# The first round of q and k projections of a fused attention and expert block, re-staged on five engines

## The chip, the cores and the metric

The kernel runs on one core of one Trainium2 chip, as a single launch. The metric is device time in microseconds from start to end of one execution; the figure of a version is the median of its runs.

## What is computed

The reference is a transformer block on 16 batches of 1024 tokens with 256 features, cut here to what matters:

```python
qkv = x @ Wqkv                                   # q, k, v: 16 heads of 16
for i in range(H):
    cos, sin = tables(i)                         # each head has its own frequencies
    q_rot, k_rot = rotary(q[:, i], cos, sin), rotary(k[:, i], cos, sin)
    att = einsum('btd,bsd->bts', q_rot, k_rot) * scale
    if i: att = att + cascade_w[i - 1] * cascade_bias
    att = softmax(where(causal, -inf, att))
    head_outputs.append(einsum('bts,bsd->btd', att, v[:, i]))
    cascade_bias = mean(att, axis=1, keepdims=True)
x = layernorm(x + concatenate(head_outputs) @ Wproj)
x = layernorm(x + mixture_of_8_experts(x))       # top 1, sigmoid weight, silu gate
```

## The kernel before

**The units.** The 256 pairs of batch and head are units. They run head after head in groups of four batches (four slots). A unit is eight steps; step by step TensorE fills scores twice (`fill_a`, `fill_b`), VectorE takes row maxima (`row_max`, L942), ScalarE takes exponentials (`exp_a`, `exp_b`), TensorE multiplies with v (`att_v`) and GpSimd works on short columns.

**The projections.** Scores come from bfloat16 stacks: q and k are each split into three bfloat16 parts, whose six products are laid one under the other in `q_stack` and `k_stack`. Eight heads of four batches make one round of projections: 16 chunks of 128 features by 512 tokens (four a batch: two of q, two of k) and eight value jobs. One chunk n goes through these stages, each named in `chunk_job`:

- `qk_a`, `qk_b` (L706, TensorE): the two halves of the product over 256 features, into a PSUM bank.
- `qk_turn` (L978 and L979, VectorE): times the cosine table into `by_cos`, and neighbouring rows exchanged into `swapped`. It frees the bank.
- `qk_sin` (L1292 and L1296, GpSimd): `swapped` times the sine table, plus `by_cos`, into one of two halves of `rotated`.
- `qk_first` (L839 on ScalarE in the first round): the first bfloat16 part.
- `qk_less` (L985, VectorE): the remainder, into one of two halves of `resid`.
- `qk_second` (L991, VectorE): the second part, a cast.
- `qk_third` (L1305, GpSimd): the third part.
- `qk_send` (L1438, queue of SP): the three parts to `qk_parts` in DRAM, from one of three buffers of `parts`.

**What sets the order.** The function `timetable` lays the stages of all jobs out in steps before a kernel instruction is made. A stage comes `gap` steps after the one before it in its job, not before those named in `after`, and, if it holds a bank, not before one is free. Each engine then issues its share of the steps in order, so a wait holds up whatever stands behind it on that engine. The first round is laid out before the units, in the steps up to `PROLOGUE`, with no unit beside it; the later rounds go between the units' steps, a chunk at a time. In the first round `by_cos` and `swapped` are single, and `qk_turn` of a chunk waits for `qk_sin` of the chunk before.

**The first stacks.** At step `PROLOGUE` SP waits until all 16 sends have landed and issues 12 loads of 16 by 4096 elements for head 0 (`load_stack`, L1375), and four short loads of zeros behind them (L1379). The first `fill_a` (L623) waits for all of these.

**The loads at the start.** SP issues 14 constants, `w_qkv` second among them (L1346), then x of batches 1 and 0 (L1431) and the cosine and sine tables. All constants count on one semaphore, which the first projection waits for. Two rooms hold x: batches 2 and 3 wait for the projections of batches 0 and 1.

## Time and profile before

| | us |
|---|---|
| median of three runs | 4006.76 |
| lowest and highest run | 4002.16, 4019.21 |
| profiled execution, its own time | 4015.91 |
| its span in the trace | 4014.0 |
| TensorE busy | 3248.6 (81%) |
| ScalarE busy | 3127.4 (78%) |
| VectorE busy | 2632.2 (66%) |
| GpSimd busy | 2175.5 (54%) |
| mean granted TensorE clock | 0.942 of full speed |

The profile cuts the span into 40 slices and gives the busy share of each engine in tenths: PE (TensorE) and ACT (ScalarE) show 5388888 and 1399999 in the first seven, so the first two slices, some 200 us, differ from what follows. The trace gives times from the start of the span. A row of its timeline has start, duration, engine, line, operation, and in brackets the idle time before and what ended it; DVE is VectorE, POOL GpSimd, and SPq an issue on SP's queue.

### The profile page before, as it was taken

What the parts mean: (1) busy time and instruction counts of PE and PEld (TensorE: products, weight loads), DVE (VectorE), ACT (ScalarE), POOL (GpSimd) and SP (SyncE); (2) the same over time, 40 slices, a digit from 0 to 9 for tenths busy, and PEclk for the clock granted to TensorE, in tenths of its full rate; (3) what the DMA queues carried; (4) which work ended last, traced back from release to release, by engine and by line L of the source; (5) the groups of instructions that cost most, each with busy time, mean ns of one, the idle gap of its engine ahead of it and who ended that gap; (6) DMA issues with size and microseconds to landing.
All of it is one profiled execution on the core that took longest, in us unless ns stands there. A gap on an engine that the chain in (4) does not pass through costs nothing. (4 is left out here: it accounts for less than half of the span.)

```text
span 4014.0 us, 86383 instructions
## 1 busy us (share of the span) xinstructions
PE 3248.6 (81%) x26666; PEld 1728.4 (43%) x26666; DVE 2632.2 (66%) x7958; ACT 3127.4 (78%) x8883; POOL 2175.5 (54%) x6232
## 2 busy tenths in 40 slices
PE   5388888888888788888888878888888888888756
PEld 2144434444444444444444434444444444444444
DVE  3466665666777667666767666667676766776546
ACT  1399999998788877778877877778887888888534
POOL 4555555555555466664554456665654534654227
PEclk8699999999999999999999999999998999999977
DMA  3333223333333433433442333443433423444245
GB/s 103 88 75 69 69 65 69 76 76 72 96 85 101 95 100 94 105 97 90 103 101 78 101 78 90 105 115 100 95 92 75 110 59 72 105 106 93 84 151 164
DMA packets 217693, 371.30 MB, mean 93 GB/s; under 512 B 45077, under 2 KB 160541, under 8 KB 204944
## 3 DMA queue, kind: packets, MB, share of 16 engines
q1 hardware_dynamic: 201872, 327.91, 32.8%
q0 software_dynamic: 15360, 37.87, 3.6%
q8 instruction: 213, 3.49, 0.4%
q14 instruction: 248, 2.03, 0.2%
HBM read 261.86 MB, written 104.92 MB: 91 GB/s over the span
## 5 line engine op out<-in xcount | busy, mean ns | idle before, releaser
L942 DVE CUSTOM_DVE_ANT_0 att_a<-scores,window 128x128 f32<-128x128 f32 (+7 forms) x2048 | 1495.1, 755 | 977.2 <-PE scores L623 700.8
L808 ACT ACTIVATE att_a<-att_a,neg_max 128x128 f32<-128x128 f32 (+7 forms) x2048 | 1576.8, 770 | 390.8 <-DVE neg_max L942 382.6
L818 ACT ACTIVATE att_t<-scores 128x1024 f32<-128x1024 f32 (+7 forms) x2048 | 1306.5, 638 | 175.8 <-PE scores L642 164.5
L640 PE MATMUL scores<-q_stack,k_stack 102*128 102x512 bf16 (+3 forms) x3072 | 833.4, 340 | 441.5 <-DVE neg_max L942 261.4
L666 PE MATMUL pv<-att_t,v_sb 128*32 128x128 f32 (+1 forms) x13312 | 893.3, 328 | 31.8 <-DVE o_sb L957 21.2
L623 PE MATMUL scores<-k_stack,q_stack 99*128 99x512 bf16 (+3 forms) x3072 | 697.7, 337 | 95.1 <-DMA k_stack<-in_zeros 59.8
L666 PEld LDWEIGHTS pv<-att_t,v_sb 128*32 128x32 f32 x13312 | 473.3, 111 | 463.0 <-issue 230.4
L640 PEld LDWEIGHTS scores<-q_stack,k_stack 102*128 102x128 bf16 x3072 | 243.6, 99 | 916.0 <-DVE neg_max L942 619.3
L642 PE MATMUL scores<-identb,mask 128*128 128x128 bf16 x2048 | 461.0, 225 | 0.0
L818 ACT ACTIVATION_READ_ACCUMULATOR att_t<-scores 128x1 f32 x2048 | 402.0, 196 | 0.1
L623 PEld LDWEIGHTS scores<-k_stack,q_stack 99*128 99x128 bf16 x3072 | 252.2, 100 | 336.0 <-issue 182.3
L808 ACT ACTIVATION_READ_ACCUMULATOR att_a<-att_a,neg_max 128x1 f32 x2048 | 390.3, 191 | 0.0
L1250 POOL TENSOR_SCALAR guess<-row_sum 128x8 f32<-128x8 int32 x256 | 51.4, 201 | 623.0 <-ACT att_a L808 612.8
L1292 POOL TENSOR_TENSOR swapped<-swapped,sine 128x512 f32<-128x512 f32 x128 | 162.9, 1273 | 293.4 <-DVE swapped L979 293.4
L706 PE MATMUL side<-xT,w_qkv 128*128 128x512 f32 x460 | 257.8, 643 | 19.2 <-DMA xT<-in_xt 15.3
L642 PEld LDWEIGHTS scores<-identb,mask 128*128 128x128 bf16 x2048 | 204.8, 100 | 100.0 <-issue 48.0
L1336 POOL DMA_INDIRECT out<-runner_r,out_id x140 | 145.5, 1039 | 101.9 <-DVE runner_r L1218 52.8
L1305 POOL TENSOR_TENSOR parts<-resid,parts 128x512 bf16<-128x512 f32 x128 | 153.3, 1199 | 73.0 <-DVE parts L991 72.7
L1329 POOL DMA_INDIRECT runner_r<-x_rows,in_id x140 | 142.4, 1017 | 77.9 <-DVE out_id L1175 36.7
L1296 POOL TENSOR_TENSOR rotated<-swapped,by_cos 128x512 f32<-128x512 f32 x128 | 163.1, 1274 | 33.1 <-DVE resid L985 14.8
L1300 POOL TENSOR_SCALAR parts<-rotated 128x512 bf16<-128x512 f32 x112 | 168.6, 1506 | 9.1
L792 PE MATMUL side<-runner_r 128*128 128x128 f32 x1040 | 154.2, 294 | 17.7 <-DVE runner_r L1200 6.2
(339 smaller groups left out, 4304.6 us busy)
## 6 DMA issues: line engine op xcount, KB each, us to landing
runner_r<-in_experts SPq DMA_DIRECT2D x140, 384.0 KB, 4.0
qk_parts<-parts SPq DMA_DIRECT2D x128, 384.0 KB, 3.1
q_stack<-qk_parts SPq DMA_DIRECT2D x384, 128.0 KB
k_stack<-qk_parts SPq DMA_DIRECT2D x384, 128.0 KB
xT<-in_xt SPq DMA_DIRECT2D x30, 1024.0 KB
head_out<-o_sb SPq DMA_DIRECT2D x252, 64.0 KB, 2.1
x_rows<-finisher_f SPq DMA_DIRECT2D x28, 514.0 KB, 4.0
finisher_f<-head_out SPq DMA_DIRECT2D x56, 256.0 KB, 4.7
```

What stands on the lines that cost most here:

```text
L623: made = engine.matmul(scores[:, c0:c1], qs[0:ROWS_A, i * P:(i + 1) * P], ks[0:ROWS_A, c0 - base:c1 - base], start=True, stop=True)
L640: engine.matmul(scores[:, c0:c1], ks[0:ROWS_B, j * P:(j + 1) * P], qs[0:ROWS_B, j * P + c0 - base:j * P + c1 - base], start=True, stop=True)
L642: engine.matmul(scores[:, base:base + P], mask[:, :], identb[:, :], start=False, stop=True, skip_group_check=True).then_inc(s_b_filled, 1)
L666: made = engine.matmul(dst, lhsT, src, start=(j == 0), stop=(p == TB - 1), skip_group_check=True)
L706: made = engine.matmul(room, w_qkv[:, k, col:col + P], xT[x_room(m)[0]][:, k, c % 2 * WB:(c % 2 + 1) * WB], start=(k == 0), stop=(k == KT ...
L792: made = engine.matmul(room[:, two * P:(two + 1) * P], r.w_gu[:, k, two, :], r.xwT[:, k * P:(k + 1) * P], start=(k == 0), stop=(k == KT - 1))
L808: engine.activation(taken, taken, EXP, scale=-1.0, bias=neg_max[:, n, i:i + 1], accum_out=row_sum[:, n, i:i + 1]).then_inc(s_exp_a, 1)
L818: engine.activation(att_t[:, ring:ring + end - base], scores[:, base:end], EXP, accum_out=col_sum[:, n, j:j + 1]).then_inc(s_exp_b, 1)
L942: engine.tensor_tensor_reduce(out=att_a[:, ring:ring + end - base], in0=scores[:, base:end], in1=window[:, T - (end - base):T], op0=ALU.ad ...
L1292: ev = small(engine.tensor_tensor(swapped[:, :], swapped[:, :], sine[:, cols], ALU.mult))
L1296: engine.tensor_tensor(rotated[:, b, :], swapped[:, :], by_cos[:, :], ALU.add).then_inc(s["qk_sin"], 1)
L1300: engine.tensor_scalar(parts[:, n % NPARTS, 0, :], rotated[:, n % 2, :], SCALE if n // 2 % 2 == 0 else 1.0, None, ALU.mult).then_inc(s["qk ...
```

## The change

It touches the first round alone and what stands around it. `first_chunk_job` replaces `chunk_job` for the first 16 chunks: gaps of one and no phases, and `qk_turn` of chunk n waits for `qk_sin` of n-2. A second pair of buffers for `by_cos` and `swapped` lies in `att_t`, which the first `exp_b` would otherwise write. The third part moves from GpSimd to VectorE, the second from VectorE to ScalarE. The loads of x move to ScalarE's queue. On SP, `w_qkv` comes first with a semaphore of its own and the other constants follow the tables; the zeros are loaded early; head 0's stacks are loaded batch by batch, each set as 12 loads of 16 by 1024 elements. Ones in the stacks are written as float32 pairs, and the scaling of `w_cas` moves to the end of the prologue.

```diff
+    def first_chunk_job(n):
+        return [Stage("qk_a", n, 0, hold=3, after=(("x_load", n // 4), ("tables", 0), ("qk_b", n - 1))),
+                Stage("qk_b", n, 1),
+                Stage("qk_turn", n, 1, frees=True, after=(("qk_sin", n - 2),)),
+                Stage("qk_sin", n, 0, after=(("qk_less", n - 2),)),
+                Stage("qk_first", n, 1, after=(("qk_send", n - NPARTS),)),
+                Stage("qk_less", n, 1), Stage("qk_second", n, 1), Stage("qk_third", n, 1), Stage("qk_send", n, 0)]
...
+        turn_bufs = [(by_cos[:, :], swapped[:, :]), (att_t[:, 0:WB], att_t[:, WB:2 * WB])]
+        def turn_buf(n):
+            return turn_bufs[n % 2 if n < 4 * SLOTS else 0]
...
-                    pe.wait_ge(s_stack[h % 2], 192 * (hh // 2 + 1))
+                    if hh == 0:
+                        pe.wait_ge(s_first[slot], 192)
+                    else:
+                        pe.wait_ge(s_stack[h % 2], 192 * (hh // 2 + h % 2))
...
-                            pe.wait_ge(s_loaded, ALL_LOADED)
+                            pe.wait_ge(s_w_qkv, 16)
...
+                    elif kind == "qk_second" and t < PROLOGUE:
+                        act.wait_ge(s["qk_less"], nth["qk_less", n])
+                        engine.copy(parts[:, n % NPARTS, 1, :], resid[:, n % 2, :]).then_inc(s["qk_second"], 1)
+                    elif kind == "x_load" and t < PROLOGUE:
+                        load_x(act, engine, n)
...
-            dve.wait_ge(s_loaded, ALL_LOADED)
-            engine.tensor_scalar(w_cas[:, :], w_cas[:, :], 1.0 / T, None, ALU.mult).then_inc(s_set_up, 1)
...
+                if t == PROLOGUE:
+                    dve.wait_ge(s_loaded, ALL_LOADED)
+                    engine.tensor_scalar(w_cas[:, :], w_cas[:, :], 1.0 / T, None, ALU.mult).then_inc(s_set_up, 1)
...
-                        if n:
-                            dve.wait_ge(s["qk_sin"], nth["qk_sin", n - 1])
+                        was = n - 2 if n < 4 * SLOTS else n - 1
+                        if was >= 0:
+                            dve.wait_ge(s["qk_sin"], nth["qk_sin", was])
...
-                    elif kind == "qk_second":
+                    elif kind == "qk_third" and t < PROLOGUE:
+                        dve.wait_ge(s["qk_second"], nth["qk_second", n])
+                        engine.tensor_tensor(parts[:, n % NPARTS, 2, :], resid[:, n % 2, :], parts[:, n % NPARTS, 1, :],
+                                             ALU.subtract).then_inc(s["qk_third"], 1)
+                    elif kind == "qk_second" and t >= PROLOGUE:
...
+            def load_first_stack(slot):
+
+                for b in range(NPARTS):
+                    sp.wait_ge(s_parts[b], 16 * len(range(b, 4 * (slot + 1), NPARTS)))
+                for n in range(2 * PRODUCTS):
+                    qk, k = divmod(n, PRODUCTS)
+                    stack, part = ((q_stack, Q_PARTS[k]), (k_stack, K_PARTS[k]))[qk]
+                    engine.dma_start(stack[k * HD:(k + 1) * HD, 0, slot, :],
+                                     qk_parts[qk, part, 0:HD, slot, :]).then_inc(s_first[slot], 16)
...
-                if t == PROLOGUE:
-                    for n in range(2 * PRODUCTS + SLOTS):
-                        load_stack(0, n)
+                if t == 1:
+                    load_constants()
+                    sp.wait_ge(s_set_up, READY)
+                    for slot in range(SLOTS):
+                        load_zeros(0, slot)
...
+                        if m < SLOTS and slot and c == 1:
+                            load_first_stack(slot - 1)
+                        if n == 4 * SLOTS - 1:
+                            load_first_stack(slot)
```

On VectorE in the steady part of the first round a chunk stands as these rows before (the turn of chunk 4, the cast of chunk 1, the remainder of chunk 2, and so on):

```order
L978 TENSOR_TENSOR by_cos<-scores,cosine 128x512 [waits s_qk_sin,s_qk_b]
L979 STREAM_SHUFFLE swapped<-scores 128x512
L991 CAST parts<-resid 128x512 [waits s_qk_less]
L985 SCALAR_TENSOR_TENSOR resid<-rotated,parts 128x512 [waits s_qk_third,s_qk_first]
L978 TENSOR_TENSOR by_cos<-scores,cosine 128x512 [waits s_qk_sin,s_qk_b]
L979 STREAM_SHUFFLE swapped<-scores 128x512
L991 CAST parts<-resid 128x512 [waits s_qk_less]
L985 SCALAR_TENSOR_TENSOR resid<-rotated,parts 128x512 [waits s_qk_third,s_qk_first]
```

and as these now (the turn of chunk 4, the third part of chunk 1, the remainder of chunk 3), with two pairs of buffers:

```order
L1018 TENSOR_TENSOR by_cos<-scores,cosine 128x512 [waits s_qk_sin,s_qk_b]
L1019 STREAM_SHUFFLE swapped<-scores 128x512
L1030 TENSOR_TENSOR parts<-resid,parts 128x512 [waits s_qk_second]
L1025 SCALAR_TENSOR_TENSOR resid<-rotated,parts 128x512 [waits s_qk_third,s_qk_first]
L1018 TENSOR_TENSOR att_t<-scores,cosine 128x512 [waits s_qk_sin,s_qk_b]
L1019 STREAM_SHUFFLE att_t<-scores 128x512
L1030 TENSOR_TENSOR parts<-resid,parts 128x512 [waits s_qk_second]
L1025 SCALAR_TENSOR_TENSOR resid<-rotated,parts 128x512 [waits s_qk_third,s_qk_first]
```

The remainder now stands one chunk nearer to the turn behind it, the third part is in the place of the cast, and the turn's wait is for a sum on GpSimd that lies one chunk further back.

On GpSimd the same stretch reads before:

```order
L1305 TENSOR_TENSOR parts<-resid,parts 128x512 [waits s_qk_second]
L1292 TENSOR_TENSOR swapped<-swapped,sine 128x512 [waits s_qk_turn]
L1296 TENSOR_TENSOR rotated<-swapped,by_cos 128x512 [waits s_small,s_qk_less]
L1305 TENSOR_TENSOR parts<-resid,parts 128x512 [waits s_qk_second]
L1292 TENSOR_TENSOR swapped<-swapped,sine 128x512 [waits s_qk_turn]
L1296 TENSOR_TENSOR rotated<-swapped,by_cos 128x512 [waits s_small,s_qk_less]
```

and now:

```order
L1337 TENSOR_TENSOR swapped<-swapped,sine 128x512 [waits s_qk_turn]
L1341 TENSOR_TENSOR rotated<-swapped,by_cos 128x512 [waits s_small,s_qk_less]
L1337 TENSOR_TENSOR att_t<-att_t,sine 128x512 [waits s_qk_turn]
L1341 TENSOR_TENSOR rotated<-att_t 128x512 [waits s_small,s_qk_less]
L1337 TENSOR_TENSOR swapped<-swapped,sine 128x512 [waits s_qk_turn]
L1341 TENSOR_TENSOR rotated<-swapped,by_cos 128x512 [waits s_small,s_qk_less]
```

The subtraction that stood ahead of each product is gone from this engine.

On SP the end of the first round, from the last sends to the next round's x and tables, reads before:

```order
L1438 DMA qk_parts<-parts 128x3x512 [waits s_qk_third] x16
L1375 DMA q_stack<-qk_parts 16x4096 [waits s_parts1,s_parts2,s_parts0,s_set_up]
L1375 DMA q_stack<-qk_parts 16x4096 x5
L1375 DMA k_stack<-qk_parts 16x4096 x6
L1379 DMA k_stack<-in_zeros 3x1024 x4
L1431 DMA xT<-in_xt 128x2x1024 [waits s_qk_b,s_v_b]
L1422 DMA cosine<-in_cos 128x1024 [waits s_qk_sin]
L1423 DMA sine<-in_sin 128x1024
```

and now, from the four sends ahead of the third batch's stack on:

```order
L1494 DMA qk_parts<-parts 128x3x512 [waits s_qk_third] x4
L1438 DMA q_stack<-qk_parts 16x1024 [waits s_parts2,s_parts1,s_parts0]
L1438 DMA q_stack<-qk_parts 16x1024 x5
L1438 DMA k_stack<-qk_parts 16x1024 x6
L1494 DMA qk_parts<-parts 128x3x512 [waits s_qk_third] x2
L1438 DMA q_stack<-qk_parts 16x1024 [waits s_parts2,s_parts1,s_parts0]
L1438 DMA q_stack<-qk_parts 16x1024 x5
L1438 DMA k_stack<-qk_parts 16x1024 x6
L829 DMA xT<-in_xt 128x2x1024 [waits s_qk_b,s_v_b]
L1484 DMA cosine<-in_cos 128x1024 [waits s_qk_sin]
L1485 DMA sine<-in_sin 128x1024
```

The loads of batches 0 to 2 stand between sends, and those of batch 3 are left between the last send and the next x.

## Rows read from the trace of the kernel before

**Rows 1.** the page: the span

```profile
span 4014.0 us, 86383 instructions
```

**Rows 2.** busy by stretch: PE, PEld, DVE, ACT, POOL; clock, DMA share

```profile
57.00:131.00 74.00, 17.63 (x37) 6.90 (x36) 31.64 (x61) 8.90 (x15) 49.39 (x37) 0.58 0.21 69
...
200.00:600.00 400.00, 344.02 (x2957) 161.45 (x2956) 242.54 (x663) 375.97 (x1079) 227.30 (x751) 1.00 0.30 70
```

**Rows 3.** timeline, one chunk of the steady stretch: start us, us, what

```profile
65.49 0.69 DVE L978 TENSOR_TENSOR by_cos<-side,cosine 128x512 f32<-128x512 f32 x1 [3.74 <-POOL rotated L1296]
...
66.10 0.72 DVE L979 STREAM_SHUFFLE swapped<-side 128x512 f32<-128x512 f32 x1
...
67.04 0.69 DVE L985 SCALAR_TENSOR_TENSOR resid<-rotated,parts 128x512 f32<-128x512 f32 x1
67.21 1.53 POOL L1305 TENSOR_TENSOR parts<-resid,parts 128x512 bf16<-128x512 f32 x1 [1.82 <-DVE parts L991]
...
68.71 1.26 POOL L1292 TENSOR_TENSOR swapped<-swapped,sine 128x512 f32<-128x512 f32 x1
...
70.11 1.26 POOL L1296 TENSOR_TENSOR rotated<-swapped,by_cos 128x512 f32<-128x512 f32 x1
71.40 0.63 ACT L839 ACTIVATE parts<-rotated 128x512 bf16<-128x512 f32 x1 [5.35 <-POOL rotated L1296]
71.47 0.69 DVE L978 TENSOR_TENSOR by_cos<-scores,cosine 128x512 f32<-128x512 f32 x1 [3.74 <-POOL rotated L1296]
```

**Rows 4.** timeline, SP's issues and the first scores

```profile
132.87 2.65 SPq L1375 DMA_DIRECT2D q_stack<-qk_parts  x6
...
139.70 0.40 SPq L1431 DMA_DIRECT2D xT<-in_xt  x1
...
147.30 1.33 PE L623 MATMUL scores<-k_stack,q_stack 99*128 99x128 bf16 x4 [59.82 <-DMA k_stack<-in_zeros]
147.60 0.29 DVE L942 CUSTOM_DVE_ANT_0 att_a<-scores,window 128x128 f32<-128x128 f32 x1 [18.55 <-PE scores L623]
```

**Rows 5.** timeline, the first x load, projection and turn

```profile
7.94 0.47 SPq L1431 DMA_DIRECT2D xT<-in_xt  x1
...
15.35 2.07 PE L706 MATMUL side<-xT,w_qkv 128*128 128x512 f32 x2 [15.35 <-DMA xT<-in_xt]
...
20.88 0.69 DVE L978 TENSOR_TENSOR by_cos<-side,cosine 128x512 f32<-128x512 f32 x1 [2.46 <-PE side L706]
```

**Rows 6.** timeline, TensorE in batch 0 and the load of batch 3

```profile
28.81 1.05 PE L720 MATMUL scores<-w_qkv,att_a 128*128 128x128 f32 x8
...
30.60 1.02 PE L706 MATMUL side<-xT,w_qkv 128*128 128x512 f32 x2
...
44.73 0.38 SPq L1431 DMA_DIRECT2D att_a<-in_xt  x1
...
50.73 1.16 PE L720 MATMUL scores<-w_qkv,att_a 128*128 128x128 f32 x8 [3.50 <-DMA att_a<-in_xt]
```

**Rows 7.** timeline, VectorE behind GpSimd, and GpSimd alone

```profile
122.53 1.44 POOL L1292 TENSOR_TENSOR swapped<-swapped,sine 128x512 f32<-128x512 f32 x1
...
122.77 1.75 DVE L985 SCALAR_TENSOR_TENSOR resid<-rotated,parts 128x512 f32<-128x512 f32 x1
...
129.13 1.15 POOL L1305 TENSOR_TENSOR parts<-resid,parts 128x512 bf16<-128x512 f32 x1 [1.09 <-DVE parts L991]
```

**Rows 8.** one line of the kernel: ns least, median, most

```profile
L978 DVE TENSOR_TENSOR by_cos<-side,cosine x117: 672/685/692, 20.9 to 3213.4; 128x512 f32<-128x512 f32 x117
```

**Rows 9.** DMA issues up to 180 us: KB, median us from issue to landing

```profile
qk_parts<-parts SPq DMA_DIRECT2D x16, 384.0 KB, 2.5
...
cosine<-in_cos SPq DMA_DIRECT2D x2, 512.0 KB, 9.7
```

**Rows 10.** timeline, the first projection of the second round

```profile
158.48 3.24 PE L706 MATMUL side<-xT,w_qkv 128*128 128x512 f32 x4
...
163.28 0.69 DVE L978 TENSOR_TENSOR by_cos<-side,cosine 128x512 f32<-128x512 f32 x1
```

More of the change, by code:

```diff
@@ L87, in block_kernel @@
     NEG = 4
+    TWO_ONES = float(np.array([0x3f803f80], np.uint32).view(np.float32)[0])
     SWAP = [i ^ 1 for i in range(32)]
@@ L287, in timetable @@
             for c in range(4):
-                begin(chunk_job(4 * slot + c))
+                begin(first_chunk_job(4 * slot + c))
             for c in range(2):
@@ L548, in block_kernel @@
         s_stack = [signal(f"s_stack{i}") for i in range(2)]
+        s_first = [signal(f"s_first{i}") for i in range(SLOTS)]
         s_shift = [signal(f"s_shift{i}") for i in range(SLOTS)]
@@ L1291, in pool_program @@
                         pool.wait_ge(s_tables, 32 * (n // 16 + 1))
-                        ev = small(engine.tensor_tensor(swapped[:, :], swapped[:, :], sine[:, cols], ALU.mult))
+                        straight, crossed = turn_buf(n)
+                        ev = small(engine.tensor_tensor(crossed, crossed, sine[:, cols], ALU.mult))
                         if n >= 2:
@@ L1295, in pool_program @@
                         pool.wait_ge(s_small, ev)
-                        engine.tensor_tensor(rotated[:, b, :], swapped[:, :], by_cos[:, :], ALU.add).then_inc(s["qk_sin"], 1)
+                        engine.tensor_tensor(rotated[:, b, :], crossed, straight, ALU.add).then_inc(s["qk_sin"], 1)
                     elif kind == "qk_first" and t >= PROLOGUE:
```

70 lines of the change are left out of this document (38 added, 32 removed).

## The prediction

> **What bounds the kernel now.** The span is 4014.0 us [rows 1]. I read the table by stretch first, because the change touches only the start: between 200 and 600 us ScalarE is busy for 376 of 400 us [rows 2], so the units pace themselves, and what they gain or lose at their start moves their end by as much. Between 57 and 131 us no engine is full: VectorE is busy for 31.6 of 74 us, GpSimd for 49.4 [rows 2]. A stretch like that is a chain of waits, so I then read the timeline of one chunk.
>
> The chain repeats every 5.98 us, from the product with cosine at 65.49 to the next at 71.47 [rows 3]. By the starts: product with cosine 0.61, exchange and cast until GpSimd's subtraction begins 1.11, subtraction 1.50, product with sine 1.40, sum 1.36 until VectorE may write `by_cos` again. The sum is 5.98, and everything in it stands in a row because there is one `by_cos`. VectorE's idle time of 3.74 us ahead of each product with cosine is that wait.
>
> At the end of the round SP issues the stacks from 132.87, the first scores start at 147.30, held by the last landing, and the first row maximum at 147.60 [rows 4]. The number to predict is this last one, called R. It is 147.6 now.
>
> **Start.** x of batch 0 is issued at 7.94 behind 14 constants; the first product starts with its landing at 15.35 and the first turn at 20.88 [rows 5]. Now `w_qkv` and x head two queues. The wait can shrink by no more than the 7.2 us by which the issue comes sooner, (7.94 to about 0.7), and could grow by 0.8 if bytes in flight set it: by the shapes 3.7 MB land up to 15.35 now, and 3.9 with the tables ahead and the other constants behind. The queue's 14 short issues are gone either way; I take 2.35 us, a third of the upper end. Ones as float32 pairs and `w_cas` at the end cost nothing: VectorE waits for TensorE there, 2.46 us before the first turn [rows 5]. If that cover went, it would still have the 5 us of the first projection.
>
> **TensorE's lead, chunks 0 to 3.** Two halves of value jobs lie between 28.81 and 30.60 [rows 6], 0.9 us each, which is 1.05 less the overlap with the next; half a projection is 1.02 less the same, 0.86, so four chunks with two value jobs are 8 x 0.86 + 4 x 0.9 = 10.5 us, or 2.6 a chunk. Projection 3 ends at 31.62 [rows 6], now at 29.3. Its turn takes 1.35 us (0.61 and 0.72 [rows 3]) and its sum is ready 2.7 us after that: 33.4. Up to there TensorE sets the pace. x of batch 2 is asked for at 29.4, and its first use comes behind turns that aren't due before 37.
>
> **Chunks 4 to 15.** With two pairs of buffers the turn of n+2 runs beside the sum of n+1. What remains is a ring of three engines, and its pace has these bounds:
> - GpSimd alone: 1.40 + 1.26 us and the start of the next, some 2.7; TensorE's 2.6 is just under it. So 2.75 a chunk is the lower bound.
> - The two engines hinder each other. VectorE's remainder takes 0.69 us [rows 3] and 1.75 when it starts 0.24 us into a GpSimd product [rows 7]; GpSimd's subtraction takes 1.15 us alone [rows 7] and 1.53 when it starts inside the remainder [rows 3]. Either waits for most of what the other has left. The product with cosine, which reads PSUM, shows 692 ns at most over 117 [rows 8], so I let it and the exchange run free. No row shows the third part on VectorE; its nearest is the remainder, the same size with one more operation, 0.69. Two such operations a chunk, with 0.1 to 0.2 us saved at each hand-over, put 1.0 us on 2.7: **3.7 us**.
> - `parts` has three buffers. From the remainder of n+1 to that of n+3 there are turn 1.35, remainder and third part 0.69 each, a send of 2.6 (2.5 from issue to landing [rows 9]), and the first part 0.63 with 0.1 of signals: 6.1 us for two chunks, 3.05 each, and up to 4.1 if both VectorE operations wait 1.06 us.
>
> I take 3.7, which both of the last two allow. Moving the cast to ScalarE removes nothing further: its copy is the size of the first part, 0.63, and ScalarE has two such a chunk. Twelve chunks give 33.4 + 12 x 3.7 = 77.8.
>
> x of batch 3 took 6.0 us from issue to first use [rows 6]. Now it is asked for after projection 7, near 42.5, which waits for a turn; it lands at 48.5 and projection 9 is done at 50.4. Its sum would begin at 51.9 by the pace. The load is hidden by 1.5 us, and not if the pace is quicker.
>
> SP issues 12 stack loads in some 5.3 us (six in 2.65 [rows 4]). Three times this stands between sends: each time the next send comes 5.8 - 3.7 = 2.1 us late, of which 0.7 to 1.1 are slack. I take 1 us each, 3 in all, between 0 and 6. So the sum of chunk 15 is ready at 80.8.
>
> Behind it come first part 0.63, remainder 0.69, second 0.6, third 0.69 and four signals: 3.1. R is **83.9**, 63.7 us sooner. The 14.4 us of stack loads that stood ahead of R are now behind it for batch 3 alone and beside other work for the rest.
>
> **What comes late next.** SP is left with the last stack's 12 issues and the landing ahead of it, so x and tables of the next round are issued 8.0 us after R; they were issued at 139.70, 7.9 us ahead of it. TensorE first wants that x at 158.48 and VectorE the table at 163.28 [rows 10], 10.9 and 15.7 us after R. With a landing of 5.5 and, for the tables, 9.7 us [rows 9], they come 2.6 and about 2.3 late. Behind TensorE's wait stand the scores of unit 1, behind VectorE's its row maxima; the two waits overlap. I charge 3 us, between 0 and 10. The fourth stack lands some 13 us after R, and unit 3 starts later than 20. TensorE's clock is 0.58 in the stretch to 131 [rows 2] and the four halves at 158.48 take 3.24 us; it might be up sooner after a shorter idle time, worth 0 to 3 us. I count none.
>
> **Sum.** 63.7 - 3.0 = 60.7 us. On the profiled execution that is 4015.9 - 60.7 = 3955.2; that one lay 9.2 us above the median of 4006.8, and by the median the forecast is **3946**. The difference is 1.5%, three times the half per cent (20 us) that a measurement of this kernel can tell.
>
> A rule speaks against two engines so closely paired. The Trainium skill (SBUF — State Buffer, "Who interferes with whom") says that a VectorE operation with two inputs in SBUF and a GpSimd operation that reads SBUF exclude each other for the whole instruction. The 1.75 us agree with it; by the letter of it a chunk would cost 1.26 + 1.26 + 0.69 + 0.69 = 3.9 us. The loads of x gain little by another rule of the Trainium skill (DMA: Bandwidth & Descriptors, "Issuing engines are not separate DMA queues"): a second queue saves issue time only. By it the start gains what the constants free, as charged.
>
> **The rivals.**
> - *Nothing overlaps at a hand-over.* The pace is 3.9, the four durations one behind the other. For it: 1.75 is a whole remainder plus 1.06 of waiting. Against: the product it waited for had 1.20 us left [rows 7], so 0.14 were saved. 12 x 0.2 = 2.4 later: 3949. Chance 0.15. The Trainium skill's page on SBUF says the same.
> - *The engines hardly meet.* The remainder falls into GpSimd's gap and the pace is 2.8. Then x of batch 3 is no longer hidden: sum 9 at 54.4, sum 15 at 71.2, R at 74.3, and 3937. Against: GpSimd would have no gap left. Chance 0.15.
> - *The ring of `parts` sets the pace.* Both VectorE waits and sends slowed behind stack loads give 4.6: 33.4 + 55.2 + 3.1 = 91.7, a gain of 55.9 - 3, so 3954; with next-round loads later by 7 us more, 3961. For it: twelve loads issued from 132.87 on had landed only by 147.30 [rows 4]. Chance 0.13.
> - *One chunk in flight, slower than before.* If the sends' landing closed the ring so that a chunk's whole chain of turn 1.35, product and sum 2.7, first 0.7, remainder 1.75, second 0.65, third 1.75, send 2.6, some 11.5 us, ran alone, R would be 18.5 + 16 x 11.5 = 202 and the kernel 4061. It decides from a pace of 8.5 us on. Against it stand two turn pairs, two halves of `rotated`, three of `parts`. Chance 0.02.
> - *The change doesn't carry through.* R comes early, but the units wait for something tied to the start of the span, and the time stays near 4000. No row shows such a thing. Chance 0.05.
>
> **How the numbers follow.** The forecast has 0.50, with 3938 to 3955 as its own range. The range of 3928 to 3964 takes in the quick pace less a clock gain, the ring with late loads, and 3 us of scatter; left out are the last two rivals and the far ends. Faster by over 0.5% is every case down to 3986.7: 0.50 + 0.15 + 0.15 + 0.13 = 0.93, and 0.01 of the last: 0.94. Same 0.04, slower 0.02.
>
> **What would show it.** First turn at 18.5; products with cosine 3.7 us apart from chunk 4 on; VectorE's remainders and third parts well over 0.69 us; the first row maximum at 84; the first projection of the second round waiting for x some 11 us behind it; the stretch beyond 200 us unchanged, only earlier. The forecast is wrong if the spacing is under 3.0 or over 4.5, or if units 1 to 4 lose over 10 us.

## The result, and the profile after it

| | before | changed |
|---|---|---|
| median, us | 4012.99 (4 runs) | 3959.61 (4 runs) |
| lowest and highest | 4002.16, 4022.01 | 3958.26, 3960.26 |
| profiled execution, its span | 4015.91, 4014.0 | 3960.26, 3958.5 |
| first row maximum, R | 147.60 | 84.45 |
| from R to the end of the span | 3866.4 | 3874.1 |

The ratio is 0.9868, with a 95% interval of 0.9839 to 0.9897: 1.3% faster, and the interval does not reach 1. One run more of the kernel before moved its median from 4006.76 to 4012.99, so the medians are 53.4 us apart and the two profiled spans 55.5. Of those spans the prologue gave 147.60 - 84.45 = 63.15 us, and what follows R took 7.65 back.

The busy times of the changed kernel, from the page:

```profile
PE 3240.7 (82%) x26666; PEld 1725.4 (44%) x26666; DVE 2638.1 (67%) x7958; ACT 3135.6 (79%) x8899; POOL 2159.7 (55%) x6216
```

They hardly differ from before: the work is the same. The difference lies in when it runs. Three stretches of the changed kernel follow, the first the pipeline, the second what stands right behind R, the third the one that [rows 2] shows for the kernel before. The columns are the stretch, its length, the busy time of each engine, the granted clock, the DMA share and GB/s.

```profile
20.00:76.90 56.90, 42.11 (x180) 24.96 (x179) 43.74 (x71) 19.96 (x36) 45.70 (x30) 0.89 0.42 134
84.45:110.00 25.55, 11.05 (x24) 3.06 (x24) 11.54 (x34) 11.65 (x29) 3.19 (x17) 0.50 0.46 143
200.00:600.00 400.00, 342.50 (x2929) 160.18 (x2928) 241.81 (x661) 373.05 (x1071) 224.41 (x744) 0.99 0.30 68
```

In the pipeline VectorE and GpSimd are now busy for 77% and 80% of the time, where they were at 43% and 67%. Behind R, TensorE works for 11 of 25.6 us. Beyond 200 us ScalarE again has 373 of 400 us: that stretch is unchanged, only earlier.

**The start.** These are rows of the timeline of the changed kernel: start, duration, engine, line, operation, and the idle time before with what ended it. They answer to [rows 5].

```profile
0.73 0.48 ACTq L829 DMA_DIRECT2D att_a<-in_xt  x1
1.25 0.52 ACTq L829 DMA_DIRECT2D xT<-in_xt  x1
14.48 2.08 PE L727 MATMUL side<-xT,w_qkv 128*128 128x512 f32 x2 [14.48 <-DMA xT<-in_xt]
20.00 0.69 DVE L1018 TENSOR_TENSOR by_cos<-side,cosine 128x512 f32<-128x512 f32 x1 [10.26 <-PE side L727]
```

The load of x that goes out first is that of batch 1, into `att_a`; batch 0, which TensorE waits for, stands behind it. The first product is 0.87 us sooner than before, though its x is asked for 6.7 us sooner. Nine kernels of this document have this start; their first products lie between 13.81 and 14.48 and their first turns between 18.48 and 20.00, so the trace shown is at the late end of both.

**One chunk.** The same view of VectorE and GpSimd in the steady part. It answers to [rows 3].

```profile
68.40 0.68 DVE L1018 TENSOR_TENSOR att_t<-side,cosine 128x512 f32<-128x512 f32 x1
...
69.01 0.72 DVE L1019 STREAM_SHUFFLE att_t<-side 128x512 f32<-128x512 f32 x1
...
69.63 0.67 DVE L1030 TENSOR_TENSOR parts<-resid,parts 128x512 bf16<-128x512 f32 x1
69.81 1.61 POOL L1337 TENSOR_TENSOR att_t<-att_t,sine 128x512 f32<-128x512 f32 x1 [0.21 <-DVE att_t L1019]
...
70.40 1.57 DVE L1025 SCALAR_TENSOR_TENSOR resid<-rotated,parts 128x512 f32<-128x512 f32 x1
71.57 1.53 POOL L1341 TENSOR_TENSOR rotated<-att_t 128x512 f32<-128x512 f32 x1
71.90 0.68 DVE L1018 TENSOR_TENSOR by_cos<-scores,cosine 128x512 f32<-128x512 f32 x1
```

The next turn comes 3.50 us after this one, and VectorE's rows carry no idle time. The remainder (L1025) takes 1.57 us where it took 0.69; it starts 0.59 into GpSimd's product with sine (L1337) and ends 0.55 after it. The product itself takes 1.61; with the third part (L1030) it shares 0.5 us. By the starts the chain is: turn 0.61, exchange and its signal 0.80, product 1.61, what the remainder has left after it 0.48. The sum is 3.50. The product for one chunk and the remainder of the chunk before stand in one row, though neither needs the other's result. This holds from the turn of chunk 4 on. The turns of chunks 1 to 3 are 3.5 us apart too, but for another reason. There VectorE is idle and waits for TensorE, for 2.17, 1.58 and 0.26 us:

```profile
23.52 0.69 DVE L1018 TENSOR_TENSOR att_t<-scores,cosine 128x512 f32<-128x512 f32 x1 [2.17 <-PE scores L727]
...
27.02 0.69 DVE L1018 TENSOR_TENSOR by_cos<-scores,cosine 128x512 f32<-128x512 f32 x1 [1.58 <-PE scores L727]
```

TensorE is busy without a gap from 20.0 to 30.5 us, with two halves of a projection (0.86 each) and two halves of value jobs (0.89 each) for every chunk, which makes 3.5 us.

**Behind the last send.** The issues on SP's queue in the changed kernel, and what waits for them. They answer to [rows 4] and [rows 10].

```profile
82.74 2.95 SPq L1438 DMA_DIRECT2D q_stack<-qk_parts  x6
85.74 2.73 SPq L1438 DMA_DIRECT2D k_stack<-qk_parts  x6
88.51 0.95 SPq L1494 DMA_DIRECT2D qk_parts<-parts  x2
92.51 2.63 SPq L1438 DMA_DIRECT2D q_stack<-qk_parts  x6
95.18 2.73 SPq L1438 DMA_DIRECT2D k_stack<-qk_parts  x6
98.02 0.39 SPq L829 DMA_DIRECT2D xT<-in_xt  x1
```

```profile
84.45 0.28 DVE L977 CUSTOM_DVE_ANT_0 att_a<-scores,window 128x128 f32<-128x128 f32 x1
...
102.90 3.78 PE L727 MATMUL side<-xT,w_qkv 128*128 128x512 f32 x4 [8.01 <-DMA xT<-in_xt]
```

The last two sends have their data by 84.5, yet they go out at 88.51, behind the 12 issues of batch 2's stack. Only when they have landed, at 92.5, do the last 12 go out, and x of the next round behind those, at 98.02, 13.6 us after R. The sends are 4.1 us late by that, and their own issue and landing take 4.0. TensorE waits 8.01 us for x, and the first projection of the second round starts 18.45 us after R instead of 10.9.

### The profile page after: what moved, and what is told of

Its sections match the earlier page's. It is cut to its first block and busy times, and to the rows that moved or that the text cites. A ratio compares the mean times of both kernels' runs of the same rounds, so it can differ in the third digit from the quotient of the medians.

```text
span 3958.5 us, 86418 instructions
## 1 busy us (share of the span) xinstructions
PE 3240.7 (82%) x26666; PEld 1725.4 (44%) x26666; DVE 2638.1 (67%) x7958; ACT 3135.6 (79%) x8899; POOL 2159.7 (55%) x6216
## 3 DMA queue, kind: packets, MB, share of 16 engines
q8 instruction: 213, 3.49, 0.4%
## 5 line engine op out<-in xcount | busy, mean ns | idle before, releaser
L1337 POOL TENSOR_TENSOR swapped<-swapped,sine 128x512 f32<-128x512 f32 x120 | 154.8, 1290 | 302.6 <-DVE swapped L1019 302.6
L977 DVE DVE_READ_ACCUMULATOR2_ANT neg_max<- 128x1 f32 x2048 | 168.2, 82 | 0.0
L1341 POOL TENSOR_TENSOR rotated<-swapped,by_cos 128x512 f32<-128x512 f32 x120 | 154.2, 1285 | 17.2
```

The costliest lines, as they stand in the source:

```text
L977: engine.tensor_tensor_reduce(out=att_a[:, ring:ring + end - base], in0=scores[:, base:end], in1=window[:, T - (end - base):T], op0=ALU.ad ...
L1337: ev = small(engine.tensor_tensor(crossed, crossed, sine[:, cols], ALU.mult))
```

## The experiments

Two theories stood against each other. **Theory A** was that of the forecast: VectorE and GpSimd hold each other up and so set the pace, and the late x is what the kernel gives back. **Theory B** had two parts: the pace is that of the sends' ring of `parts` or of the stack loads between the sends, and the time lost after R comes from the batch-wise stacks themselves.

Kernels 1 to 4 ran on one chip, where the kernel before took 4013.52 us; 5 to 8 on a second, where its one run took 4086.15; 9 to 11 on a third, where it took 4062.71. The pace repeats on all three, to some 0.02 us. R scatters more: the unchanged change has 84.45 and 83.61, and kernel 1, whose issues are the same up to its last send, has 81.79. So the pace is compared across all, a difference in R of less than 3 us between two kernels shows nothing, and whole times are compared only with the kernel before on the same chip. Kernels 2 to 8 have one time each.

### 1. x of the next round ahead of the last stack

```diff
                         if n == 4 * SLOTS - 1:
+                            load_x(sp, engine, SLOTS)
+                            load_tables(1)
                             load_first_stack(slot)
```

> The x and the two tables of the second round are issued on SP between the last send and the last stack, instead of behind it. Theory (the units lose 7.6 us after the first row maximum, because TensorE waits 8.0 us for this x with the scores of unit 1 queued behind it): the first row maximum stays at 84.5, the second round's first projection starts 10 to 12 us behind it instead of 18.4, and the span falls by 6 to 8 us against the changed kernel, to about 3951. Rival (the units would have lost the time anyway, to a low TensorE clock or to the late fourth stack): the projection starts sooner, but the span falls by less than 2 us.

R was 81.79 and not 84.5: its first turn came at 18.48, and the rest lies within the scatter. The issue of x and the projection in this kernel's timeline:

```profile
87.26 0.38 SPq L829 DMA_DIRECT2D xT<-in_xt  x1
...
93.24 2.08 PE L727 MATMUL side<-xT,w_qkv 128*128 128x512 f32 x2 [1.03 <-DMA xT<-in_xt]
```

TensorE's wait falls from 8.01 to 1.03 us, and the projection starts 11.45 us after R. To see what that is worth I took the GpSimd operation that ends each unit's row sums (`guess`), here of unit 8, in the kernel before, the changed one and this one:

```profile
263.81 0.20 POOL L1250 TENSOR_SCALAR guess<-row_sum 128x8 f32<-128x8 int32 x1
```

```profile
210.31 0.20 POOL L1294 TENSOR_SCALAR guess<-row_sum 128x8 f32<-128x8 int32 x1
```

```profile
200.93 0.20 POOL L1294 TENSOR_SCALAR guess<-row_sum 128x8 f32<-128x8 int32 x1
```

Counted from R these are 116.2, 125.9 and 119.1 us. The change lost 9.7 us there, and the order of two loads and a stack gives back 6.8 of them. The median was 3954.59 us (3943.21 to 3964.20), a ratio to before of 0.9841 [0.9816, 0.9867], whose interval overlaps that of the change. So the mechanism is shown at unit 8, and the gain in whole time by this edit alone is not. Its profiled execution was the slowest of the four. By unit 96 the 6.8 us, counted from R, have shrunk to 0.9, while two executions of the unchanged change (the second is kernel 11) differ by 3.6 there. TensorE's granted clock falls in some stretches among the units, as to 0.83 between 320 and 340 us here, 0.85 there in the changed kernel and 0.91 between 480 and 500 in the kernel before. I put the loss of the lead down to such stretches, which is argued and not tested.

### 2. Stacks loaded whole, behind all sends

```diff
+                if t == PROLOGUE:
+                    for n in range(2 * PRODUCTS):
+                        load_stack(0, n)
...
-                        if m < SLOTS and slot and c == 1:
-                            load_first_stack(slot - 1)
-                        if n == 4 * SLOTS - 1:
-                            load_first_stack(slot)
```

> Head 0's stacks are again loaded whole, 12 loads of 16 by 4096, behind all 16 sends; everything else as changed. Theory (the pace of 3.5 us is set by VectorE and GpSimd, and the stack loads between sends cost about 1 us each and 4 to 5 in all): turns stay 3.5 us apart from chunk 4 to 15, the last third part is ready about 4 us sooner, near 80, and the first row maximum comes 17 us behind it, near 97, 13 us later than now. Rival (the ring of three send buffers sets the pace of itself): turns are 3.9 apart even without stack loads, and the first row maximum is near 101.

```profile
84.60 2.63 SPq L1420 DMA_DIRECT2D q_stack<-qk_parts  x6
...
99.30 0.29 DVE L974 CUSTOM_DVE_ANT_0 att_a<-scores,window 128x128 f32<-128x128 f32 x1 [17.57 <-PE scores L641]
```

R is 99.30, 14.9 us later than with the batch-wise loads. The pace stays at 3.50, and the last turn comes at 74.19 instead of 77.00. From first turn to last it is 54.36 us, against 57.00, 56.40 and 55.86 in the three executions with batch-wise stacks (the changed kernel, kernels 11 and 1): the 36 issues between the sends cost 1.5 to 2.6 us. Without them the turns of chunks 9 and 10 still come 1.6 us late in all, behind a TensorE that waits 3.47 us for x of batch 3. Unit 8 ends its row sums 117.4 us after R. But x of the next round is issued ahead of R here, as in the kernel before, so this kernel alone can't tell the stacks from the late x. Kernel 9 can: it has batch-wise stacks, four loads at a time, and x in time, and nothing is lost after R. The one time was 3973.35 us.

### 3. The third part almost left out

The third part is computed for 8 of its 512 columns and is zero in the others, so its time on VectorE goes and everything else stays.

```diff
-                        engine.tensor_tensor(parts[:, n % NPARTS, 2, :], resid[:, n % 2, :], parts[:, n % NPARTS, 1, :],
+                        engine.tensor_tensor(parts[:, n % NPARTS, 2, 0:8], resid[:, n % 2, 0:8], parts[:, n % NPARTS, 1, 0:8],
```

> In the first round the third part is taken of 8 of 512 columns only, the others are left zero, so VectorE has one two-input operation a chunk instead of two. Theory (in the steady part VectorE and GpSimd take the SBUF port in turn, and VectorE is never free: products 0.61, exchange 0.62, third part 0.78, remainder 1.50 with its wait, 3.5 in all): the product with sine starts 0.35 sooner and takes 1.26 instead of 1.61, and the pace falls to 2.8 to 2.9 us, where TensorE sees to it that it falls no further. Rival (send ring or signals): the pace stays over 3.3.

```profile
66.51 0.68 DVE L1019 TENSOR_TENSOR att_t<-side,cosine 128x512 f32<-128x512 f32 x1
...
67.75 0.14 DVE L1031 TENSOR_TENSOR parts<-resid,parts 128x8 bf16<-128x8 f32 x1
67.92 1.26 POOL L1338 TENSOR_TENSOR att_t<-att_t,sine 128x512 f32<-128x512 f32 x1 [0.21 <-DVE att_t L1020]
...
68.41 1.32 DVE L1026 SCALAR_TENSOR_TENSOR resid<-rotated,parts 128x512 f32<-128x512 f32 x1 [0.52 <-ACT parts L871]
...
69.66 0.68 DVE L1019 TENSOR_TENSOR by_cos<-scores,cosine 128x512 f32<-128x512 f32 x1
```

The pace is 3.15, between what the two theories gave. VectorE lost 0.53 us of work and now idles for 0.52, so its own load no longer sets the pace. The product fell from 1.61 to 1.26, and the pace by the same 0.35: turn 0.61, exchange and signal 0.80, product 1.26, rest of the remainder 0.48. The third part thus costs the pipeline 0.35 us a chunk, and only through GpSimd's product. R was 81.47, only 3 us sooner and hardly outside the scatter: some chunks took 4.56, and the first three gaps stayed at 3.5 to 3.9, as they would where TensorE sets them. The one time was 3953.41 us.

### 4. One pair of turn buffers

```diff
         def turn_buf(n):
-            return turn_bufs[n % 2 if n < 4 * SLOTS else 0]
+            return turn_bufs[0]
```

with `qk_turn` waiting for `qk_sin` of n-1 again, in the stage list and in VectorE's wait.

> One pair of turn buffers instead of two, with the wait for the sum of the chunk before, and all else as changed. Theory (the second pair is the main part of the gain in pace): the ring is product 0.61, exchange and third part 1.3, sine and sum 2.7 with a port wait of 0.35, and 0.1 of signals, 5.0 us a chunk, so the first row maximum comes 12 x 1.4 = 17 us later, near 101. Rival (moving the subtraction off GpSimd was the main part): the pace is under 4.3 us and the first row maximum before 95.

```profile
60.68 0.69 DVE L1018 TENSOR_TENSOR by_cos<-side,cosine 128x512 f32<-128x512 f32 x1 [1.23 <-POOL rotated L1341]
...
62.10 1.61 POOL L1337 TENSOR_TENSOR swapped<-swapped,sine 128x512 f32<-128x512 f32 x1 [1.52 <-DVE swapped L1019]
...
63.85 1.53 POOL L1341 TENSOR_TENSOR rotated<-swapped,by_cos 128x512 f32<-128x512 f32 x1
...
65.49 0.69 DVE L1018 TENSOR_TENSOR by_cos<-scores,cosine 128x512 f32<-128x512 f32 x1 [1.23 <-POOL rotated L1341]
```

The chain is that of [rows 3] without GpSimd's third part: 1.42 + 1.75 + 1.64 = 4.81 a chunk. R was 96.96, 12.5 later than with two pairs; the one time was 3970.86 us. The expectation had 5.0 and an R of 101. In this order the parts that the change moves to other engines take 1.17 us off the chunk of before (5.98 to 4.81), and the second pair takes off 1.31 more (to 3.50).

### 5. The third part back on GpSimd

```diff
-                    elif kind == "qk_third" and t >= PROLOGUE:
+                    elif kind == "qk_third":
```

on GpSimd, and VectorE's branch for it taken out.

> The third part of the first round goes back to GpSimd; two turn pairs and all else as changed. Theory (engines take the port in turn): GpSimd has 1.15 + 1.26 + 1.36 of its own and waits for most of a remainder of 0.69, so the pace is 4.2 to 4.5 us instead of 3.5, and the first row maximum comes 9 to 12 us later, near 95. Rival (no port, only GpSimd's own work): 3.8 us, near 88.

```profile
70.79 0.69 DVE L1025 SCALAR_TENSOR_TENSOR resid<-rotated,parts 128x512 f32<-128x512 f32 x1 [3.97 <-POOL parts L1346]
...
71.40 0.68 DVE L1018 TENSOR_TENSOR by_cos<-scores,cosine 128x512 f32<-128x512 f32 x1
...
72.81 1.26 POOL L1333 TENSOR_TENSOR swapped<-swapped,sine 128x512 f32<-128x512 f32 x1 [2.12 <-DVE swapped L1019]
74.22 1.27 POOL L1337 TENSOR_TENSOR rotated<-swapped,by_cos 128x512 f32<-128x512 f32 x1
...
75.44 1.16 POOL L1346 TENSOR_TENSOR parts<-resid,parts 128x512 bf16<-128x512 f32 x1
...
76.70 0.69 DVE L1025 SCALAR_TENSOR_TENSOR resid<-rotated,parts 128x512 f32<-128x512 f32 x1 [3.97 <-POOL parts L1346]
```

The pace is 5.91 and R 111.45: nearly that of before, with two turn pairs. What I expected added durations and overlooked an order. The remainder of chunk n overwrites `resid`, so it waits for the third part of n-2. On GpSimd that stands behind the sum, the turn stands behind the remainder on VectorE, and the product needs the turn. One file: remainder 0.61, turn and exchange with the signal 1.41, product 1.41, sum 1.22, third part 1.26. That is 5.91, and no operation is slowed by another here. The one time was 4050.67 us, 35.5 under the one run of the kernel before on this chip. So the second pair of buffers gives next to nothing to the pace without the move of the third part.

Yet R is 36.2 us sooner than before. Only 1.4 of them come at the first turn and 0.7 in the ten chunks after the sixth turn. 17.7 us lie behind the last turn, where the whole stacks stood, and 16.3 between the first and the sixth turn. These last come from a stop in the kernel before, whose turns of chunks 4 and 5 are 16.8 us apart:

```profile
56.22 0.58 ACT L848 COPY v_sb<-scores 128x512 f32<-128x512 f32 x1 [11.81 <-PE scores L720]
...
57.37 0.69 DVE L985 SCALAR_TENSOR_TENSOR resid<-rotated,parts 128x512 f32<-128x512 f32 x1 [13.03 <-ACT parts L839]
```

ScalarE waits for values of batch 3, whose x TensorE has only at 50.73 ([rows 6]), and the first parts and all behind them wait with it. In the new layout of the first round this stop is gone, here as in the changed kernel. Which edit of the layout ended it was not tested.

### 6. The cast back on VectorE

```diff
-                    elif kind == "qk_second" and t < PROLOGUE:
-                        act.wait_ge(s["qk_less"], nth["qk_less", n])
-                        engine.copy(parts[:, n % NPARTS, 1, :], resid[:, n % 2, :]).then_inc(s["qk_second"], 1)
...
-                    elif kind == "qk_second" and t >= PROLOGUE:
+                    elif kind == "qk_second":
```

> The second part of the first round goes back to VectorE as a cast, the third part stays there. In the changed kernel VectorE is without a gap in the steady part, so the cast adds its 0.33 to 0.41 us and, where it meets a GpSimd operation, up to 1 us of waiting: a pace of 3.9 to 4.5 and a first row maximum 5 to 12 us later. The prediction held that moving it removes nothing; by that the pace stays 3.5.

```profile
70.91 1.61 POOL L1334 TENSOR_TENSOR att_t<-att_t,sine 128x512 f32<-128x512 f32 x1 [1.88 <-DVE att_t L1016]
71.32 1.48 DVE L1032 CAST parts<-resid 128x512 bf16<-128x512 f32 x1
...
72.66 1.26 POOL L1338 TENSOR_TENSOR rotated<-att_t 128x512 f32<-128x512 f32 x1
72.72 1.75 DVE L1022 SCALAR_TENSOR_TENSOR resid<-rotated,parts 128x512 f32<-128x512 f32 x1
```

The cast takes 1.48 us inside GpSimd's product; in the chunk of [rows 3] it starts at 66.72 and takes 0.41. Behind it the remainder meets the sum and takes 1.75. VectorE now waits out both of GpSimd's operations, and the pace is 4.90, over the 3.9 to 4.5 that I had expected. R was 97.23, the one time 4030.56 us (55.6 under before). Moving the cast to ScalarE is worth 12.8 us of R, as much as the second pair of buffers.

### 7. x of batch 0 first

```diff
-                        load_x(act, engine, n)
+                        load_x(act, engine, 1 - n if n < 2 else n)
```

> Of the first two loads of x, that of batch 0 is issued first, and that of batch 1 behind it. Theory (bytes in flight set the landing, 1 MB takes 2.5 to 3 us at 360 to 400 GB/s): the first product starts near 11.8 instead of 14.5, the first turn near 17.5, and the first row maximum 2 to 2.7 us sooner. Rival (w_qkv is what the first product waits for, or a fixed delay): within 1 us of 14.5.

```profile
8.68 2.07 PE L727 MATMUL side<-xT,w_qkv 128*128 128x512 f32 x2 [8.68 <-DMA xT<-in_xt]
```

The first product starts at 8.68 instead of 14.48, the first turn at 14.00 instead of 20.00, more than I had expected (11.8 and 17.5). R is 78.31, 5.3 and 6.1 us under the two of the unchanged change, so what the start gains reaches R. The one time was 4020.24 us, 65.9 under before.

### 8. Stack loads four at a time

```diff
-                        if m < SLOTS and slot and c == 1:
-                            load_first_stack(slot - 1)
+                        if m < SLOTS and slot and c:
+                            load_first_stack(slot - 1, 4 * (c - 1), 4 * c)
```

> The 12 loads of each of the first three stacks are issued four at a time behind three sends instead of all at once. Theory (SP's 5.6 us of issues hold the next send back, and with three buffers the first part of a chunk then waits): turns 9 to 15 stay 3.5 to 3.6 us apart, and the first row maximum comes 3 to 4 us sooner, near 81. Rival (the loads slow the sends in the DMA engines, whoever issues them when): the same stretches, less than 1.5 us sooner.

The last turn comes at 73.44 and R at 80.89, 3.6 us sooner than in the change. From first turn to last it is 54.00 us, 1.9 to 3.0 less than with the loads all at once; the rest of the 3.6 is scatter of the start. x of the next round is issued at 92.50, still behind the last stack, and TensorE waits 6.14 us. The one time was 4020.00 us, 66.2 under before.

### 9 to 11. All three together, and the change again

Kernel 9 has the edits of 1, 7 and 8. Kernel 10 has them too, with x of the next round already behind send 13:

```diff
+                        if n == 13:
+                            load_x(sp, engine, SLOTS)
```

Kernel 11 is the changed kernel again, without an edit.

> Three edits on the changed kernel together: x of batch 0 ahead of batch 1, stack loads four at a time behind three sends, and x and tables of the second round ahead of the last stack. If the terms add, as the engines' order lets them (5.5 us at the start, 3.5 of the held sends, 7 to 9 of the late x): first row maximum near 75.5, unit 8 another 7 us or more sooner against it, and a span 15 to 18 us under the changed kernel's on the same chip. Rival (clock dips of TensorE in the units take back what the start gives): the first row maximum and unit 8 come sooner as said, but the medians differ by less than 8 us.

> As the one before, with the second round's x issued after send 13 instead of 15. Theory (in that one x comes just in time or 1 us late): the second round's first projection doesn't wait for x any more, and the tables are then what is late, so unit 8 gains 0 to 2 us more. Rival (1 MB in the DMA engines between the sends holds sends 14 and 15 back): the first row maximum comes 2 to 3 us later, and no gain is left.

> The changed kernel as it is, on the same chip as the two before, so that the medians can be compared. By both theories the first row maximum is at 84 to 85 and the ratio to the kernel before is 0.985 to 0.989.

| | R | projection after R | TensorE's wait | unit 8 | median, us | ratio to before [95%] |
|---|---|---|---|---|---|---|
| 9, all three | 76.22 | 10.7 | 0.28 | 192.4 | 3995.14 | 0.9830 [0.9812, 0.9848] |
| 10, x earlier | 75.49 | 10.2 | none | 194.0 | 3994.04 | 0.9828 [0.9812, 0.9844] |
| 11, the change | 83.61 | 18.5 | 8.06 | 208.4 | 4015.74 | 0.9878 [0.9857, 0.9898] |

The projection of the second round in the timeline of kernel 9, whose x is issued at 82.03:

```profile
86.94 2.93 PE L727 MATMUL side<-xT,w_qkv 128*128 128x512 f32 x3 [0.28 <-DMA xT<-in_xt]
```

Kernels 9 and 10 are 20.6 and 21.7 us under the change on the same chip, and their intervals against the kernel before do not meet that of the change. In kernel 9 unit 8 stands at R + 116.2, where the kernel before had it too: 7.4 us of R and 8.6 after it make 16.0. The other 5 are within the scatter. With the still earlier x of kernel 10 R is 0.7 us sooner, which is within its scatter, and unit 8 is at R + 118.5; the two can't be told apart by their times. In both the first turn now waits for the table of sines, which lands after x.

## Why the prediction came out as it did

**Right: what bounded the kernel, and what the change takes away.** R was forecast for 83.9 and came at 84.45; the gain of the prologue was put at 63.7 and is 63.15. ScalarE's share beyond 200 us did not move, as the argument from [rows 2] had it. Of the 63.15 us, 0.9 come at the first turn, 20.8 between the first and the sixth turn (where the kernel before has the stop shown under 5), 20.6 in the ten chunks after it and 20.8 behind the last turn.

That R was met within 0.55 us is in part luck, since misses cancel. The sum of chunk 3 was forecast for 33.4 and is ready at 35.25, 1.85 late. The twelve chunks behind it take 46.4 us instead of 47.4: the pace gives 2.4 and the stops take 1.4. The end from the last sum to R is 2.76 instead of 3.1.

**Start: the term was rather large.** It was put at 2.35 us. In the trace shown it is 0.87 to the first product and 0.88 to the first turn; over the nine kernels with this start it is 0.9 to 1.5 and 0.9 to 2.4 (the kernel before has one trace). The forecast took a third of the upper end by choice. Neither bound saw the cause: I read the change as x at the head of a queue, and it is x of batch 1 that is at the head. Kernel 7 shows that 5.1 to 5.8 us more were there for a swap.

A rule of the Trainium skill (DMA: Bandwidth & Descriptors, "Issuing engines are not separate DMA queues") says that a second issuing engine saves only the time of issuing. By it the start could gain at most the 6.7 us by which x is issued sooner. The trace agrees, with 0.87. The swap within one queue is worth several times as much.

**Pace: right in size, and the sum behind it wrong in one term.** It was put at 3.7 from the fourth chunk on and is 3.50. The forecast built it on GpSimd's two operations plus 1.0 for the two VectorE operations that meet them. The rows show a ring: turn, exchange, product, rest of the remainder. The third part acts in it only by the 0.35 us that it puts on the product, as kernel 3 shows. TensorE sets the pace up to chunk 3, as the forecast had it, but at 3.5 us a chunk and not at 2.6: the sum counted four halves of value jobs for four chunks, and the trace has eight. R did not feel this, because the forecast took the end of projection 3 from its row in [rows 6]. Over all 16 chunks and eight value jobs 2.6 is the mean.

**The cast: wrong.** "Moving the cast to ScalarE removes nothing further" priced the copy on ScalarE and not what the cast would cost on VectorE. Kernel 6 gives the price of leaving it: 1.40 us a chunk. It had been cheap in the kernel before, where nothing ran on GpSimd beside it (GpSimd's idle time of 1.82 us in [rows 3]).

**Left out: the move of the third part.** I counted it as a cost, one more VectorE operation that meets GpSimd. Kernel 5 shows that without it the second pair of buffers gains 0.07 us a chunk. The forecast came out because the change does both, and that is luck as far as this term goes.

**Rivals of the pace.** *Nothing overlaps*, 3.9: near in kind. VectorE's two and GpSimd's two operations do alternate without a gap, and three times a chunk one starts inside the other. The remainder meets 1.02 us of the product and takes 1.57 where 0.69 + 1.02 would be 1.71; the product meets 0.49 of the third part and loses 0.35; the sum meets 0.40 of the remainder and loses 0.27. That saves 0.14, 0.14 and 0.13, and 3.90 - 0.41 is 3.49. *The engines hardly meet*, 2.8: never, the closest is 3.15 with the third part out. *The ring of `parts`*, 4.6: it shows at single places, as in the row below, but does not set the steady pace.

```profile
59.08 0.63 ACT L871 ACTIVATE parts<-rotated 128x512 bf16<-128x512 f32 x1 [3.26 <-DMA qk_parts<-parts]
```

*One chunk in flight*: the turns are 3.5 us apart, so two or more were in flight throughout.

The Trainium skill (SBUF — State Buffer, "Who interferes with whom") says that a VectorE operation with two inputs in SBUF and a GpSimd operation that reads SBUF contend for a port that one of them holds alone, and counts a cast among those that may contend. The cast's 1.48 and the remainder's 1.57 us agree in kind. In size the waits of [rows 7] and of the chunk shown are some 0.14 us shorter than a full wait.

**Loads.** The stack issues between sends were put at 3 us, between 0 and 6: kernel 2 gives 1.5 to 2.6. x of batch 3 was forecast for issue at 42.5 and first use without a wait as long as the pace was 3.7. It was issued at 43.67, and TensorE waited for it:

```profile
49.23 1.16 PE L741 MATMUL side<-w_qkv,att_a 128*128 128x128 f32 x8 [3.02 <-DMA att_a<-in_xt]
```

The turns of chunks 10 and 11 come 4.66 and 4.93 us after those before them. The first of these waited for TensorE and so for x; the second comes with the row of the ring above, whose send stood behind the stack issues of 50.73:

```profile
56.48 0.69 DVE L1018 TENSOR_TENSOR by_cos<-scores,cosine 128x512 f32<-128x512 f32 x1 [1.06 <-PE scores L727]
```

The turn of chunk 15 comes 5.10 after the one before. Together that is 4.2 us over the pace, of which kernel 2 keeps 1.6 for x of batch 3. The prediction had said that the load is no longer hidden if the pace is quicker.

**The term that was mis-sized: "What comes late next".** I charged 3 us, between 0 and 10, and 7.65 were lost over the whole span, 9.7 by unit 8. The mechanism was the one named: x of the next round stands behind the last stack on SP. Its size was off, since the forecast had x issued 8.0 us after R and it was issued 13.6 after. I had counted the last stack's issues and a landing, and not the stack before, whose 12 issues start at 82.74, in front of sends 14 and 15. They hold the sends until 88.51, where their data is there by 84.5, and everything behind them is late by as much: 4.1 of the 5.6 us. Most of the rest is the landing of those sends, 4.0 from issue where I had some 2.7. I had priced those issues only where they hold the chunks up, not where they hold up the end of the queue. Kernel 1 shows that this was the cause: with x issued 5.5 us after R instead of 13.6, TensorE's wait is 1.03 us.

The other kernels bear it out, 3 to 6 among them, which are not in the table. Counted from R, what unit 8 loses follows how late the projection is, and some 0 to 3 us are left over:

| kernel | projection later than before, us | unit 8 later than before, us |
|---|---|---|
| changed | 7.6 | 9.7 |
| 11, the change again | 7.6 | 8.6 |
| 7 | 8.4 | 9.5 |
| 8 | 5.7 | 6.6 |
| 1 | 0.6 | 2.9 |
| 2 | 0.0 | 1.2 |
| 9 | -0.2 | 0.0 |
| 10 | -0.7 | 2.2 |

**The clock.** I counted nothing for it, between 0 and 3 gained. In the 25.55 us behind R the changed kernel shows a granted clock of 0.50, that is the lower level of 1.2 GHz, where the kernel before has 0.67, and the four halves of the first projection take 3.78 us where [rows 10] has 3.24. So it was a small loss. The idle time of 8 us is not needed for it: kernel 1 waits only 1.03 us and has 0.52 and 3.78 as well. From R to unit 8 TensorE is busy for 94.2 us in the changed kernel and 94.6 in kernel 1, against 91.8 before and 91.6 in kernel 9. That is as much as most of what is left over in the table, but kernel 11 has 92.0 there beside a rest of 1.0, so this cause is likely and not shown.

**The time.** In spans the gain was forecast at 60.7 us and is 55.5: 0.55 missed at R, and 4.65 behind it. On the profiled execution that is 3955.2 against 3960.26. By the median it was 3946 against 3959.61, 13.6 us late. The other 8.5 have no mechanism: the profiled execution of before lay 9.2 us above the median then shown, and that of the change 0.65 above its own.

## What to carry to other kernels

When a pipeline gets a second buffer, look at each engine's own order as well as at its load: a wait on n-2 that stands behind another operation of the same engine (kernel 5) can close the ring again, and short operations that cost nothing beside an idle engine (kernel 6) cost a whole wait beside a busy one.

When work is moved forward on a queue, write down the queue's issues to the end, and ask what now stands in front of each send and of the next stage's loads. The edits of kernel 9, which beats this change, move no work between engines. They put x ahead of what is wanted later, and cut a block of 12 issues into pieces that fit between two sends.

## What the runs showed of the hardware

- **An issue can take eight times as long behind large loads.** SP issues most of the constants in 0.43 to 0.58 us each. `w_gate`, 32 KB, took 3.78 us and `prefix`, 64 KB, took 1.85, where each took 0.47 in the kernel before. By the sizes of the loads 4.5 MB had been asked for ahead of `w_gate` (x, `w_qkv`, the tables and constants); in the kernel before it was 1.4 MB. Kernels 1 to 11 all show the same two, at 3.2 to 4.1 and 1.5 to 2.1. What holds them was not tested.

```profile
5.46 3.78 SPq L1391 DMA_DIRECT2D w_gate<-in_gate  x1
...
9.28 1.85 SPq L1391 DMA_DIRECT2D prefix<-in_prefix  x1
```

- **Two queues share, and the order within one decides.** x of batch 0 and x of batch 1 are 1 MB each. x of batch 0 is in use at 8.68 us as the first in its queue (kernel 7) and at 13.81 to 14.48 as the second, beside the same loads on SP's queue.
- **The same kernel differs between chips by more than the change.** The same kernel before took 4013.5, 4062.7 and, in a single run, 4086.2 us on three chips, 1.8% apart, while the pace of the changed chunks stays at 3.50. The changed kernel kept its ratio: 0.9868 and 0.9878.
